# Residual rows written to the output early, finished rows added onto them by accumulating transfers, and the end of a tile placed between the next tile's low parts on VectorE

## The reference

```
x = x + ga * attention(h)                       # the residual row x
h = layernorm(x) * (1 + cb) + sb
scores = sigmoid(h @ gate_w + bias); the 2 best of 8 experts, weights normalised
for each chosen expert e: eo = gelu(h @ up_w[e] + up_b[e]) @ down_w[e] + down_b[e]
y = 0.1 * (gelu(h @ sw_up + sb_up) @ sw_down + sb_down) + sum(weight_e * 0.1 * eo)
y = y / (max(abs(y)) + 1e-6)                    # over the 256 channels of a row
out = x + gb * y
```

## Time and profile before

| | us |
|---|---|
| three timed executions | 1046.93, 1047.86, 1051.92 |
| the profiled execution | 1051.68 |
| its span | 1049.9 |
| TensorE busy | 875.8 (83%) |
| VectorE busy | 687.6 (65%) |
| ScalarE busy | 479.1 (46%) |
| GpSimd busy | 378.8 (36%) |
| mean granted TensorE clock | 0.929 |

### The profile page before, as it was taken

How to read it: one execution, slowest core, us unless ns; L and a number is a source line. 1 busy time by engine, 2 the same in 40 slices (tenths; PEclk the granted TensorE clock), 3 DMA queues, 4 the chain that set the end, 5 groups by cost and what they waited for, 6 DMA issues and landing times. The chain is left out here.

```text
span 1049.9 us, 21570 instructions
## 1 busy us (share of the span) xinstructions
PE 875.8 (83%) x5989; PEld 802.6 (76%) x5990; DVE 687.6 (65%) x1771; ACT 479.1 (46%) x879; POOL 378.8 (36%) x407
## 2 busy tenths in 40 slices
PE   6899997489989989998469889869988999889860
PEld 5687786468877867877469888869888988888860
DVE  5687874568777867876736666666666666666651
ACT  4566552134544434444354545554555445455530
POOL 3625301113244144143303444434444444444432
PEclk9899999579999999999879999989999999999995
DMA  8020000302022022022752333523333332333321
GB/s 289 25 81 1 1 1 28 133 1 78 7 84 83 2 84 83 0 84 83 248 193 74 93 91 101 168 61 98 101 101 97 87 86 80 99 101 102 104 65 36
DMA packets 60920, 87.39 MB, mean 83 GB/s; under 512 B 19269, under 2 KB 49169, under 8 KB 60720
## 3 DMA queue, kind: packets, MB, share of 16 engines
q0 software_dynamic: 15040, 44.09, 13.6%
q1 hardware_dynamic: 44464, 41.12, 12.8%
q10 hardware_dynamic: 1344, 1.31, 0.4%
HBM read 54.35 MB, written 41.55 MB: 91 GB/s over the span
## 5 line engine op out<-in xcount | busy, mean ns | idle before, releaser
L1659 PE MATMUL psUp<-eT,wup 128*128 128x256 f32 x1632 | 218.7, 297 | 56.7 <-DVE eT L1769 52.1
L1659 PEld LDWEIGHTS psUp<-eT,wup 128*128 128x128 f32 x1632 | 212.0, 205 | 63.4 <-issue 63.4
L1679 PE MATMUL psE<-wdn,gTh 128*128 128x256 f32 x1088 | 198.0, 284 | 0.0
L1679 PEld LDWEIGHTS psE<-wdn,gTh 128*128 128x128 f32 x1088 | 168.1, 191 | 0.0
L1728 ACT ACTIVATE gu<-psUp,ubias 128x256 f32<-128x256 f32 x272 | 113.9, 470 | 117.2 <-DVE gTl L1775 57.3
L1775 DVE TENSOR_TENSOR gTl<-gu,gTh 128x512 fp32r<-128x512 f32 x136 | 92.2, 698 | 107.9 <-ACT gTh L1733 104.5
L1679 PE MATMUL psE<-wdn,gTl 128*128 128x256 f32 x544 | 153.2, 282 | 0.0
L1866 POOL DMA_INDIRECT shared_x_part<-ys,widx x68 | 67.2, 988 | 179.2 <-issue 88.1
L1036 PE MATMUL psU<-h2T,su 128*128 128x512 f32 x384 | 105.4, 411 | 9.6 <-ACT gf L1118 9.6
L1855 POOL DMA_INDIRECT gx<-shared_x_part,meta x68 | 73.6, 1082 | 95.3 <-DMA shared_x_part<-ys,widx 69.9
L1679 PEld LDWEIGHTS psE<-wdn,gTl 128*128 128x128 f32 x544 | 103.6, 190 | 0.0
(11 more groups left out here) (265 smaller groups left out, 1430.7 us busy)
## 6 DMA issues: line engine op xcount, KB each, us to landing
hin<-expert_in SPq DMA_DIRECT2D x36, 256.0 KB, 2.7
X<-in_L_attn_x SPq DMA_DIRECT2D x8, 512.0 KB, 7.5
shared_x_part<-prow SPq DMA_DIRECT2D x8, 512.0 KB, 6.2
shared_x_part<-X SPq DMA_DIRECT2D x8, 512.0 KB
shared_x_part<-sh SPq DMA_DIRECT2D x7, 512.0 KB, 3.3
raw_up<-in_L_ffn_up_w SPq DMA_DIRECT2D x3, 1024.0 KB, 5.9
raw_dn<-in_L_ffn_down_w SPq DMA_DIRECT2D x3, 1024.0 KB, 9.4
expert_in<-prow SPq DMA_DIRECT2D x8, 272.0 KB, 7.1
```

Of the source, the lines that this page charges most:

```text
L1659: mm = nc.tensor.matmul(psU[:, c, (m % 2) * TR:(m % 2 + 1) * TR], wup[s][:, a, k, m * P:(m + 1) * P], eT[:, u, b, k], start=(n == 0), stop ...
L1679: mm = nc.tensor.matmul(psE[:, u, h * C:(h + 1) * C], (gTh, gTl)[a][:, u, m, h * P:(h + 1) * P], wdn[s][:, b, m], start=(n == 0), stop=(n ...
```

## The change

Residual rows go straight to `out` in stage two. `shared_x_part` becomes `shared_part`, with two slots a token. In stage three POOL scatters `fin` with `compute_op=ALU.add` onto the rows in `out`, the addition L1825 is gone, and `gx` has two slots.

On DVE a tile's end is cut in pieces: targets and `yc` stay in body j, but `bs`, `sm`, `top` and `fin` of tile j move into body j+1, `top` behind the first `gTl` and `fin` behind the second. Where no further tile is needed, `last` does what is left. `ahead` is called twice: the up weights at the body's start, the down weights ahead of `targets` (DVE) or of `ys` (ACT).

```
-    sx = nc.dram_tensor("shared_x_part", (N, 3 * C), F32, kind="Internal").ap()
+    sx = nc.dram_tensor("shared_part", (N, 2 * C), F32, kind="Internal").ap()
...
-    xr_v = sx[:, C:2 * C].rearrange("(p t) c -> p t c", t=NT)
+    xr_v = out[0].rearrange("(p t) c -> p t c", t=NT)
...
-    def tiles(eng, body):
+    def tiles(eng, body, last=None):
...
             for j in range(FULL, ET):
+                if last is not None:
+                    with unneeded(eng, j):
+                        last(j)
                 nest.enter_context(needed(eng, j))
                 body(j, j % 2, j + 1 < ET, j // 2)
+            if last is not None:
+                last(ET)
...
# PE
-                        pe.wait_ge(w_ok, 2 * k_exp + 2)
+                        pe.wait_ge(w_ok, 2 * k_exp + 1)
...
             def down(j, u, more, i):
 
                 slot = entry(pe, stab, j, 2)
+                k_exp = entry(pe, ktab, j, E)
...
+                        pe.wait_ge(w_ok, 2 * k_exp + 2)
...
# ACT
             def body(j, u, more, i):
-                ahead(j)
+                ahead(j, (0,))
                 if more:
                     gelu(j + 1, 1 - u)
                     high(j + 2, u)
+                ahead(j, (1,))
                 part_out(j, u, i)
...
# DVE
+            def end(j, u, more):
+
+                if more:
+                    low_g(j + 1, 1 - u, 0)
+                if later(j, 1):
+                    largest(j - 1)
+                if more:
+                    low_g(j + 1, 1 - u, 1)
+                if later(j, 1):
+                    gated(j - 1, 1 - u)
+                if more:
+                    low_g(j + 1, 1 - u, 2)
+                if more:
+                    low_g(j + 1, 1 - u, 3)
...
             def body(j, u, more, i):
-                ahead(j)
+                if later(j, 1):
+                    total(j - 1, 1 - u, 32 * i + 32 * u)
+                ahead(j, (0,))
                 if more and isinstance(j, int) and j + 1 >= FULL:
                     with needed(dve, j + 1):
-                        low_g(j + 1, 1 - u)
-                    low(j + 2, u)
-                elif more:
-                    low_g(j + 1, 1 - u)
+                        end(j, u, True)
+                    with unneeded(dve, j + 1):
+                        end(j, u, False)
+                else:
+                    end(j, u, more)
+                if more:
                     low(j + 2, u)
+                ahead(j, (1,))
+                targets(j, u, i)
                 result(j, u, i)
...
# POOL
                 if later(j, 2):
-                    wait(pool, f_ok, j - 1)
+                    wait(pool, s_ok, 2 * j - 2)
...
-                wait(pool, f_ok, j + 1)
+                wait(pool, f_s, 2 * j + 2)
                 for h in range(2):
...
-                                                 bounds_check=N - 1, oob_is_err=False).then_inc(o_st[u], 16)
+                                                 bounds_check=N - 1, oob_is_err=False, compute_op=ALU.add).then_inc(o_st[u], 16)
```

More of the change, by code:

```diff
@@ L882, in weights, with split_hi @@
         sp.dma_start(raw_dn[:], down_v[bass.ds(e, 1)].rearrange("a p k n -> p (a k) n")).then_inc(dn_in, 16)
-    def split_hi(act, n, s):
-        for i in range(2):
+    def split_hi(act, n, s, which=(0, 1)):
+        for i in which:
             wait(act, (up_in, dn_in)[i], 16 * n + 16)
@@ L892, in split_hi, with split_lo @@
                 nc.scalar.copy(dst[:, at], src[:, at]).then_inc(w_hi, 1)
-    def split_lo(dve, n, s):
-        for i in range(2):
+    def split_lo(dve, n, s, which=(0, 1)):
+        for i in which:
             src = (raw_up, raw_dn)[i][:].rearrange("p k n -> p (k n)")
@@ L1697, in _, with ahead @@
         def _(act):
-            def ahead(j):
+            def ahead(j, which):
                 e = entry(act, ntab, j, E - 1)
@@ L1707, in ahead @@
                         with act.If_eq(act.to_reg(slot), 1 - s):
-                            split_hi(act, k + 1, s)
+                            split_hi(act, k + 1, s, which)
             def high(j, u):
@@ L1764, in ahead @@
                         with dve.If_eq(dve.to_reg(slot), 1 - s):
-                            split_lo(dve, k + 1, s)
+                            split_lo(dve, k + 1, s, which)
             def low(j, u):
@@ L1782, in targets @@
                     wait(dve, o_st[u], 32 * i)
-                tok, third, hi = [meta[:, u, :, n:n + 1].rearrange("p h a -> p (h a)") for n in (E + 1, E + 2, E + 3)]
+                tok, half, hi = [meta[:, u, :, n:n + 1].rearrange("p h a -> p (h a)") for n in (E + 1, E + 2, E + 3)]
                 nc.vector.tensor_scalar(own[:], iota_h[:], rowf[:, bass.ds(j, 1)], None, ALU.add).then_inc(ix_c, 1)
@@ L1787, in targets @@
                 wait(dve, ix_c, 2 * j + 2)
-                nc.vector.scalar_tensor_tensor(widx[:, u], sec[:], float(BIG), third, ALU.mult, ALU.add).then_inc(ix_ok, 1)
+                nc.vector.scalar_tensor_tensor(widx[:, u], sec[:], float(BIG), half, ALU.mult, ALU.add).then_inc(ix_ok, 1)
                 nc.vector.scalar_tensor_tensor(oidx[:, u], sec[:], -float(BIG), tok, ALU.mult, ALU.add).then_inc(ix_ok, 1)
[L1791 to L1795, removed]
             def result(j, u, i):
                 e = entry(dve, etab, j, E - 1)
-                targets(j, u, i)
                 wait(dve, ey_mm, j + 1)
@@ L1805, in result, with total @@
                                         dbias[:, bass.ds(e, 1), :].broadcast_to([P, 2, C]), ALU.add).then_inc(ey_ev, 1)
-                base(j, u, i)
+            def total(j, u, landed):
+                e = entry(dve, etab, j, E - 1)
+                wait(dve, g_in[u], landed)
+                if later(j, 1):
+                    wait(dve, s_ok, 2 * j)
+                nc.vector.tensor_tensor(bs[:], gx[:, u, :, C:2 * C], gx[:, u, :, 0:C], ALU.add).then_inc(b_ok, 1)
                 wait(dve, ey_ev, j + 1)
@@ L1842, in _ @@
             dve.wait_ge(io_ok, 1)
-            tiles(dve, body)
+            tiles(dve, body, last)
         @block.gpsimd
```

39 lines of the change are left out of this document (23 added, 16 removed).

## The result

The changed kernel took 1044.62 us (median of 18, 1041.66 to 1046.6), the kernel before, on the same chip, 1049.51 us (median of 18, 1045.58 to 1052.92). The ratio is 0.9955, 95% interval 0.9943 to 0.9968: 4.9 us faster, where 8.7 slower was forecast. The sign was wrong. The interval still excludes no change at all, so a small gain is measured.

The account below looks back on a forecast made before the run. The prediction took a third-stage ring of DVE and ACT that never waits for PE as the bound. Terms 2.5 - 1 - 1.5 + 9.0 - 0.3 = +8.7 on 1047.86 gave 1056.5 us, range 1039 to 1068.

Parts of the forecast that it names:

- The mechanism: Third-stage loop: DVE and ACT form a ring; reads ahead of `yc` lose 1.55 us, 1.45 returns behind the first gelu.
- its own case: The forecast itself as one of four outcomes: 1051 to 1062 us, chance 0.55.
- the step on which the forecast rested: DVE's queue in the loop: it stands still while `eT` waits, so two table reads cost 1.55 us a tile.
- the loop tile's term: Third-stage loop: period 13.95 us, +0.1 a tile, +2.5 over some 27 tiles, bounds -4 and +13.
- The floor of 13.7: Loop period if ACT's own pace sets the fourth gelu: 13.7 us, 0.25 below the 13.95 taken.
- the rival of 1045 to 1050: Ring stays, interleaving does better: ACT's floor reached, faster small DVE instructions, accumulate landing as a plain write; chance 0.2.
- The weight splits: Two of 34 tiles: splitting in two halves partly covers DVE's work; -1 us for both, between -3 and +2.
- The written-out tiles: Tiles 1, 30 and 31, with constant waits and a shorter queue: -0.5 us each, -1.5, between -3 and +1.
- The tail: Chain of the last tiles: later `fin`, tests and accumulating landings, less residual work and gather bytes; +9.0 us in sum.
- Stage two: Last residual store goes in long runs, not 1 KB pieces: -0.3 us, between -1 and +0.5.
- The hidden reads: Rival: DVE's queue reads while `eT` waits; gelu at 5.85, next `eT` at 12.4, about 1016 us, chance 0.1.
- The accumulating scatter as the new wait: Rival: slower landing or issue lengthens the tail by 6 to 9 more and delays loop gathers; 1062 to 1075, chance 0.15.

Follow-up runs that it names:

- e1: The full change, but VectorE's second `ahead` reuses the two table entries read by the first; 0.9652 of the kernel before.
- e6: The full change's new order alone, with the residual gathered and added on VectorE as before and a plain output scatter; 0.9978 of the kernel before.
- e3: The full change with its output scatter plain instead of accumulating, the residual left out; 0.9927 of the kernel before.
- e9: e6 with the edit of e1, so new order, table entries read once on VectorE, residual as before; 0.9811 of the kernel before.
- e5: The full change, but tiles 31 and later finish their rows at once, behind their own `yc`; 0.9897 of the kernel before.
- e12: e11 plus VectorE's read of the tile's expert from `etab` moved to the body's start; 0.9497 of the kernel before.
- e7: The full change with two further unused table reads on VectorE between `eT` and `yc`; 1.0333 of the kernel before.
- e11: e1 and e5 together, plus ScalarE's three table reads moved ahead of its wait for `yc` in every second loop tile; 0.9496 of the kernel before.

## Why the prediction was wrong

The time lies in the range given for 8 in 10, 1039 to 1068, but on the other side of the kernel before.

**The mechanism was right.** Most signs that it named for its own case came: `eT` to `yc` 3.64 (3.8 forecast), first gelu 7.21 (7.4), no wait of the gelu for the first `gTl`, PE still waiting for `eT`, the scatter of tile 31 5.7 later (5.5). Two did not: the period is 13.63 and not 13.95, and the output scatter lands in 3.8 to 3.9 in the tail and not in 3.4. That the reads cannot hide behind a waiting `eT` was the step on which the forecast rested. The reads' starts and e1 show it. By the Trainium skill's rule (Perfetto Trace Analysis, section "DVE / Act Engine Instruction") the sequencer is ready for the next instruction as soon as one has been pushed into the wait queue, and the reads would hide. The traces do not agree: in the full change and in e6 the first read begins right behind the end of what `eT` waits for, and a part is hidden only in e6, where the engine still has earlier work by then.

**The step that failed is the loop tile's term.** It was forecast at +0.1 us a tile and is -0.345, outside its own bounds (13.7 to 14.35 for the even body, which takes 13.63). Over 25 tiles that is 11 us, and it alone turns the sign. The term is a small difference of two large ones, 1.55 lost in front and 1.45 got back behind, and both were off in the same direction:
- in front, 1.55 was read from the engine's starts around the reads. They begin 0.1 before `eT` does, and so run beside its own 0.68 of work; `yc` moved by 1.37, and by 1.25 between e1 and the full change;
- behind, I took the second `gTl` at 2.1 behind the first and it is 1.86 (838.34 to 836.48). `top`'s first small instruction is 0.17 long, where it was 0.44 in the tile of the earlier trace rows (the row stands below). So the gelus come to within 0.1 of ACT's own pace, and from the first gelu to the next `eT` it is 6.42 where 6.55 was counted. (The forecast's own sum, 11.9 + 2.12, is 14.02; it took 13.95.) The floor of 13.7, which the rival of 1045 to 1050 named, was nearly the right value, and I called it unlikely since "all three must come together";
- I carried the gain of the even body to both. The odd body went from 14.26 to 13.89, -0.37, where the even one went -0.24.

```profile
819.00 0.44 DVE L1817 TENSOR_SCALAR top<-top 128x2 f32<-128x2 f32 x1 [0.16 <-DVE top L1815]
```

In before this instruction took 0.30 to 0.45 in 26 of 34 tiles, each time with GpSimd busy with the issue of a transfer for the whole of it; in after it takes 0.17 in all 34, and in 32 of them GpSimd is idle. No run changed this alone.

**The weight splits:** -1 was forecast for both. The loop's pair gave -2.3, of which 0.7 is what any two tiles of the loop gave, so the split itself gave some -1.6. The other one is not told apart from the tiles around it. That is within the bounds. **The written-out tiles:** -1.5 forecast; tile 0 to 4, with the other split in it, and 31 to 33 gave -1.8 together.

**The tail** was sized well. From `eT` of tile 33 to the last scatter it took +9.7: tile 31's `fin` +5.7 (5.5 forecast), tile 32 +1.9 (1.8), tile 33 -0.7 (-0.7), landings +1.35 and +1.14 (1 each), gathers -0.7 and -0.8 (-0.6 together). The issue on POOL, 0.6 longer each of three times, was not in my sum. After the last scatter 2.2 were gained: the closing instruction of GpSimd is 6.1 long and was 8.2. It is 6.1 in all ten kernels whose output scatter accumulates and 8.2 in all four with a plain one (before, e3, e6, e9), and e3 differs from the full change in nothing else. So it comes with the accumulation; by what way is open. That the tail's lateness is this large and in the open, e5 shows: 0.6% given back.

**Stage two** gained nothing that the traces show: in e5 to e12 the first `eT` of the third stage lies between 524.8 and 531.3, whether stage two is as before (e6, e9) or as after.

**The rivals.** The hidden reads: refuted, e1 and e7. What they would have been worth was sized well: e1, without them, has its first gelu at 5.97 and a period of 12.4, where that rival had 5.85 and 12.4. The accumulating scatter as the new wait: refuted, of the 20.7 us for which `bs` waits for its gather 18.7 are in the tail's chain and 2.0 in the loop, and e3 is worth 3 us. "The ring stays and the interleaving does better": two of its three parts came, the floor and the shorter small instructions. The third did not, since the accumulate does not land as a plain write; the gain after the last scatter, which no rival had, stands in its place. So 1044.6 lies beside its 1045 to 1050 partly by luck.

## What to carry to other kernels

Where engines close a ring, price a moved step by what it puts between the ring's own instructions, its table reads above all: a read of a register from a table is hidden while the engine still has earlier work, and costs all of its time where the engine has just been waiting for another. If a forecast is the small difference of a loss and a gain of nearly the same size, its sign is open. Here the gain went to within 0.1 of the next engine's floor. Work that is moved into the next tile comes late in the last ones: write these out as they were.

## What the runs showed of the hardware

- A read of a table entry into a register by VectorE's queue took 0.30 to 0.31 us and 0.19 more of register work, 0.6 to 0.7 from one read to the next. None, two and four of them put `own` 0.62, 1.85 and 2.99 behind `eT`.
- The first such read behind `eT` began right behind the end of ACT's high part, for which `eT` waits: 827.6 behind 827.58 in the full change, 814.7 behind 814.69 in e6.
- ScalarE's three such reads took 2.1 us between `ys` and the gelu (e11), and the profile put this idle time down to TensorE.
- An accumulating indirect scatter of 128 rows of 1 KB held GpSimd 1.6 us where the plain one held it about 1.0, and landed in 3.8 to 3.9 us where the plain one took 2.4 to 2.7 in the same place of the chain. Over all 68 the medians are 3.5 and 3.0.
- GpSimd's closing instruction took 6.1 us in the ten kernels with accumulating output scatters and 8.2 in the four with plain ones.
- A small VectorE instruction got longer in some of the tiles in which it ran beside GpSimd's issue of a transfer, and in no others: `top`'s first, 0.17 us alone, took up to 0.45 in before; `own`, 0.23 us, took 0.42 in eight even bodies of e3.
- Two `gTl` shown as one row "x2" run back to back: VectorE was behind with work there (e6), and its queue began its read some 0.5 before `eT`, against 0.1 in the full change.
